# Projection with rotation by permutation, row mask inside the maximum, first loads moved ahead

## The chip, the cores and the metric

The kernel runs on one core of a Trainium2 chip. The metric is the device time in microseconds of one execution; lower is better. Engines are named as in the profile: PE is TensorE's matmul, PEld its weight load, DVE VectorE, ACT ScalarE, POOL GpSimd, SP SyncE.

## What is computed

One transformer layer over 4096 positions of width 256 in float32: causal attention with 16 heads of 16, rotary position encoding on queries and keys, then a gated feed-forward part with hidden width 1024, each followed by a layer norm.

```python
q, k, v = split_heads(x @ Wq.T + bq), split_heads(x @ Wk.T + bk), split_heads(x @ Wv.T + bv)
# rope: Y * cos + concat([-Y[..., d//2:], Y[..., :d//2]]) * sin
q, k = rope(q), rope(k)
att = softmax(where(tril, q @ k.T / sqrt(16), -inf))
x = layernorm(x + (att @ v) @ Wo.T + bo)
x = layernorm(x + ffn(x))
```

## The kernel before

The kernel is a sequence of blocks, each with its own programs for the five engines; a block starts when all engines have ended the one before. The blocks are `project`, `attend`, `widen` and `narrow`. The change touches the first two.

**`project`** (L57 to L235) works on 8 chunks of 512 positions. For each chunk it makes four column blocks of 128 features (two of the queries, two of the keys), transposed: features on partitions, positions along the free dimension. For each block PE makes two products from the chunk's x: the plain one and the rotated one, the latter with weights whose halves were exchanged and negated beforehand (`wqr`, `wkr`, made by DVE at L170 and L171). DVE then computes, in order and each step after the one before: `t1` = (plain + bias) x cos (L187), `t2` = (rotated + bias) x sin (L189), `full` = t1 + t2 (L193), and a split of `full` into three bfloat16 parts whose sum is `full` (L197 to L204). SP stores the three parts to HBM (L226). After every two blocks PE makes the values of half a chunk (L152), DVE adds their bias (L209), SP stores them (L230). Weights, biases and chunks are loaded on ACT's queue (L108 to L125). ACT computes nothing here, and GpSimd only fills the ones beside the values.

**`attend`** (L290 to L598) goes through four groups of four heads ("quads"), each with 8 chunks of queries. For one quad the queries and keys stand in SBUF as "stacks": six products of bfloat16 parts laid under one another (6 x 16 = 96 partitions), below them three partitions for the negated row maximum (queries) against ones (keys). There are two kinds of products. A row unit (`row_unit`, L454) has queries on partitions and up to 512 keys along the free dimension, and DVE reduces it to a maximum (`segment`, L531). A key unit (`key_unit`, L470) has keys on partitions, includes the subtraction of the maximum by the three extra partitions, and ACT exponentiates it (L595); its result is the moving operand of the product with the values (L489). Row units run ahead of key units by a number of columns that `rows_before_keys` lays down; the order on PE is written out by hand from it. Before the first key unit, 51 row units stand. Row units use a ring of four PSUM banks, key units of three.

A unit on the diagonal has a causal mask. In the row unit it is a second matmul of 128 columns that adds -1e30 in PSUM (L457, `mask` against `ident`); its width is 128, 256, 384 or 512 columns, depending on the tile (`row_width`). Key units have such a matmul too (L473).

When all row units of a chunk are done, `finish` (L534) splits the maxima into three parts (L541 is the first cast), PE transposes them (L448), and SP sends them through HBM into the query stack (`store_max`).

At the start of the block SP loads the stacks of the first chunk of quad 0 (twelve DMAs, `load_first`), the constants `ident` and `mask`, and the stacks of chunks 1 and 2. POOL loads the values, clears a pad of 15 columns (L367) and writes the ones into the key stacks by memset (L369), for both buffers in turn. PE waits for the casts of the constants (L558, L559) and for both pads. Later stacks of quad 0 are loaded by SP in the course of the block, three chunks ahead.

Of the kernel before, what the change touches and what calls it, by code (L numbers as in the profile page):

```python
# [18 lines left out]
F32 = mybir.dt.float32  # L19
F32R = mybir.dt.float32r  # L20
BF16 = mybir.dt.bfloat16
# [4 lines left out]
P = 128  # L26
# [22 lines left out]
FIRST_AHEAD = 3  # L49
# [7 lines left out]
def project(nc, io, qp_d, kp_d, v_d):  # L57

    with ExitStack() as ctx:
# [6 lines left out]
        wq = sb("wq", [P, DH, D])  # L66
        wk = sb("wk", [P, DH, D])
        wv = sb("wv", [P, DH, D])
        wqr = sb("wqr", [P, DH, D])
        wkr = sb("wkr", [P, DH, D])  # L70

        bias = sb("bias", [P, 4 * DH])
        sign = sb("sign", [P, 1])
        bv = sb("bv", [P, D])
        xt = sb("xt", [P, 2, DH, CH])
        cos = sb("cos", [P, 2, CH])
        sin = sb("sin", [P, 2, CH])
        t1 = sb("t1", [P, CH])
        t2 = sb("t2", [P, CH])
        full = sb("full", [P, CH])  # L80
        rest = sb("rest", [P, CH])
        parts = sb("parts", [P, 2, PARTS, CH], BF16)
        vals = sb("vals", [P, 2, 2, HEADS, VW])
        main_ps = [ctx.enter_context(nc.psum_tensor(f"pr_main{i}", [P, CH], F32)) for i in range(2)]
# [3 lines left out]
        weights_loaded = sem("weights_loaded")  # L88
        x_loaded = [sem(f"x_loaded{u}") for u in range(2)]
        tables_loaded = [sem(f"tables_loaded{u}") for u in range(2)]  # L90
        v_ones = sem("v_ones")
        weights_ready = sem("weights_ready")
        pair_ready = sem("pair_ready")
        pair_taken = sem("pair_taken")
        v_ready = sem("v_ready")
        v_taken = sem("v_taken")
        step = sem("step")
        parts_ready = sem("parts_ready")
        parts_stored = [sem(f"parts_stored{s}") for s in range(2)]
        v_stored = [sem(f"v_stored{s}") for s in range(2)]  # L100
        PAIRS = 2 * DH

        block = ctx.enter_context(nc.Block())

        @block.scalar
        def _(act):
            for dst, src in ((wq, "WqT"), (wk, "WkT"), (wv, "WvT")):
                act.dma_start(dst[:, :, :], io[src].rearrange("(c p) o -> p c o", p=P)).then_inc(weights_loaded, 16)  # L108
            act.dma_start(bias[:, :], io["bias"]).then_inc(weights_loaded, 16)
            act.dma_start(sign[:, :], io["sign"]).then_inc(weights_loaded, 16)  # L110
            act.dma_start(bv[:, :], io["bv"].partition_broadcast(P)).then_inc(weights_loaded, 16)

            def load(u, n):
                act.dma_start(xt[:, u, :, :], io["xT"][n]).then_inc(x_loaded[u], 16)
                act.dma_start(cos[:, u, :], io["cos"][n]).then_inc(tables_loaded[u], 16)
                act.dma_start(sin[:, u, :], io["sin"][n]).then_inc(tables_loaded[u], 16)

            load(0, 0)
            load(1, 1)
            with act.Fori(0, NCH // 2 - 1) as it:  # L120
                for u in range(2):

                    act.wait_ge(v_ready, it * 4 + 2 * u + 2)
                    act.wait_ge(pair_taken, it * 2 * PAIRS + PAIRS * (u + 1) + 2)
                    load(u, it * 2 + (2 + u))  # L125
# [4 lines left out]

        @block.tensor
        def _(pe):
            pe.wait_ge(weights_ready, 6)
            with pe.Fori(0, NCH // 2) as it:
                for u in range(2):
                    pe.wait_ge(x_loaded[u], it * 16 + 16)
                    for i, (w, wr) in enumerate(((wq, wqr), (wk, wkr))):
                        for half in range(DH):
                            cols = slice(half * P, (half + 1) * P)

                            pe.wait_ge(pair_taken, it * 2 * PAIRS + PAIRS * u + DH * i + half + 1)
                            for bank, weight in ((main_ps[half], w), (rot_ps[half], wr)):
                                for c in range(DH):
                                    last = nc.tensor.matmul(bank[:, :], weight[:, c, cols], xt[:, u, c, :],
                                                            start=(c == 0), stop=(c == DH - 1))
                            last.then_inc(pair_ready, 1)

                        pe.wait_ge(v_taken, it * 4 + 2 * u + i + 1)
                        for j in range(2):
                            tile = slice((2 * i + j) * P, (2 * i + j + 1) * P)  # L150
                            for c in range(DH):
                                last = nc.tensor.matmul(v_ps[i][:, j, :], xt[:, u, c, tile], wv[:, c, :],  # L152
                                                        start=(c == 0), stop=(c == DH - 1))
                        last.then_inc(v_ready, 1)

        @block.vector
        def _(dve):
            dve.sem_inc(pair_taken, 2)
            dve.sem_inc(v_taken, 2)
            dve.wait_ge(weights_loaded, 6 * 16)  # L160

# [53 lines left out]
        def _(sp):  # L215
            for s in range(2):
                sp.sem_inc(parts_stored[s], 48)
                sp.sem_inc(v_stored[s], 32)
# [1047 lines left out]
```

## Time and profile before

| | us |
|---|---|
| median of three runs | 2890.32 |
| lowest and highest | 2888.95, 2891.99 |
| profiled execution, its own time | 2888.47 |
| its span, first to last instruction | 2886.7 |

| stretch | what runs |
|---|---|
| 0 to 173.8 us | `project` |
| 173.8 to about 1800 | `attend` |
| from there to 2886.7 | end of `attend`, `widen`, `narrow` |

| engine | busy us | share of the span |
|---|---|---|
| PE | 2781.7 | 96% |
| DVE | 1944.8 | 67% |
| ACT | 1296.6 | 45% |
| POOL | 94.8 | 3% |

Times in the rows below are microseconds from the start of the span, unless a column says ns. An engine is busy while an instruction of it runs; matmuls overlap, and their ends are modelled, so a matmul's own duration is longer than the distance to the next one's start. ACTq and SPq are DMA issues of these queues. In brackets stands idle time before an instruction and what ended it.

### The profile page before, as it was taken

The page shows a single profiled execution, that of the slowest core. Times are in us where ns is not written, and L with a number is a line of the kernel's source. Part 1 is how long each engine was busy: PE and PEld are TensorE (multiplying, and loading weights), DVE is VectorE, ACT ScalarE, POOL GpSimd, SP SyncE. Part 2 cuts the span into 40 slices and gives each one's busy share as a digit, 9 for nine tenths or more (in the row PEclk, how much of TensorE's full clock was granted, in tenths as well). Part 3 has the DMA queues.
Part 4 walks back from the last instruction along what each step waited for, and adds up shares of the span by engine and source line. Part 5 has one row for each costly group of instructions (what it writes and reads, how often), then busy time and mean ns, then how long its engine had stood idle before and what let it go on. Part 6 is the DMA issues. An engine that isn't in the chain of part 4 may idle for free. (4 is left out here: it accounts for less than half of the span.)

```text
span 2886.7 us, 39857 instructions
## 1 busy us (share of the span) xinstructions
PE 2781.7 (96%) x15456; PEld 1474.2 (51%) x15456; DVE 1944.8 (67%) x3592; ACT 1296.6 (45%) x2545; POOL 94.8 (3%) x121
## 2 busy tenths in 40 slices
PE   8949999999999999999999999899999999999998
PEld 4423333333333333333333333388888887888887
DVE  7979999988888887888887776353333333344343
ACT  0005666677776676777777777511112111101100
POOL 0030100002000010000000000000000000000000
PEclk9969999999999999999999999999999999999999
DMA  5540270008000017000001000221111132112100
GB/s 155 166 106 27 45 89 3 3 2 103 7 3 4 5 28 91 3 3 3 3 3 38 18 4 8 75 71 56 57 59 64 48 124 111 44 44 87 44 15 23
DMA packets 94569, 132.89 MB, mean 46 GB/s; under 512 B 30688, under 2 KB 68192, under 8 KB 90688
## 3 DMA queue, kind: packets, MB, share of 16 engines
q1 hardware_dynamic: 83184, 96.91, 10.4%
q0 software_dynamic: 5472, 23.34, 6.5%
q10 hardware_dynamic: 5744, 10.36, 1.2%
q8 instruction: 110, 1.80, 0.3%
q14 instruction: 59, 0.48, 0.1%
HBM read 83.25 MB, written 47.32 MB: 45 GB/s over the span
## 5 line engine op out<-in xcount | busy, mean ns | idle before, releaser
L531 DVE TENSOR_REDUCE at_segmax<-at_row 128x1 f32<-128x512 f32 (+3 forms) x2304 | 1329.1, 638 | 236.2 <-PE at_row L454 178.3
L595 ACT ACTIVATE at_probs<-at_key 128x512 f32<-128x512 f32 (+3 forms) x2304 | 1130.9, 567 | 532.6 <-PE at_key L470 362.3
L454 PE MATMUL at_row<-fr_k_stack,fr_q_stack 96*128 96x512 bf16 (+3 forms) x1152 | 407.3, 374 | 32.2 <-POOL at_values L367 28.3
L470 PE MATMUL at_key<-fr_q_stack,fr_k_stack 99*128 99x512 bf16 (+3 forms) x1152 | 414.7, 364 | 2.7 <-ACT at_probs L595 2.7
L454 PE MATMUL at_row<-at_k_stack,at_q_stack 96*128 96x512 bf16 (+3 forms) x1152 | 412.1, 364 | 1.4 <-DVE at_segmax L531 1.2
L470 PE MATMUL at_key<-at_q_stack,at_k_stack 99*128 99x512 bf16 (+3 forms) x1152 | 402.8, 364 | 6.7 <-ACT at_probs L595 6.2
L489 PE MATMUL at_o<-at_probs,at_values 128*32 128x512 f32 (+3 forms) x2304 | 286.9, 570 | 0.0
L489 PE MATMUL at_o<-at_probs,fr_values 128*32 128x512 f32 (+3 forms) x2304 | 286.4, 569 | 0.0
L454 PEld LDWEIGHTS at_row<-fr_k_stack,fr_q_stack 96*128 96x128 bf16 x1152 | 112.1, 99 | 309.2 <-DVE at_segmax L531 202.1
L454 PEld LDWEIGHTS at_row<-at_k_stack,at_q_stack 96*128 96x128 bf16 x1152 | 112.0, 97 | 293.2 <-DVE at_segmax L531 211.1
L1128 ACT ACTIVATE na_h3f<-na_h,na_hs 128x512 f32<-128x512 f32 x64 | 44.1, 690 | 401.9 <-PE na_h L1098 401.9
L1098 PE MATMUL na_h<-na_h_h,fr_h2w_h 128*128 128x512 f32 x512 | 203.7, 398 | 5.4 <-DVE na_h_l L1143 5.4
L1098 PE MATMUL na_h<-na_h_l,fr_h2w_h 128*128 128x512 f32 x512 | 203.4, 397 | 0.0
L1098 PE MATMUL na_h<-na_h_h,fr_h2w_l 128*128 128x512 f32 x512 | 203.4, 397 | 0.0
L897 PE MATMUL wi_f<-wi_h_h,wi_h1w_h 128*128 128x512 f32 x512 | 201.4, 393 | 0.0
L897 PE MATMUL wi_f<-wi_h_l,wi_h1w_h 128*128 128x512 f32 x512 | 199.3, 389 | 0.0
L897 PE MATMUL wi_f<-wi_h_h,wi_h1w_l 128*128 128x512 f32 x512 | 199.3, 389 | 0.0
L1150 DVE CAST na_h_h<-na_h3f 128x512 fp32r<-128x512 f32 x64 | 27.3, 427 | 245.8 <-ACT na_h3f L1128 245.8
L941 ACT ACTIVATE wi_h<-wi_f,fr_hs 128x512 f32<-128x512 f32 x64 | 44.1, 689 | 324.6 <-PE wi_f L897 324.6
L470 PEld LDWEIGHTS at_key<-at_q_stack,at_k_stack 99*128 99x128 bf16 x1152 | 111.6, 98 | 146.9 <-ACT at_probs L595 78.8
L897 PE MATMUL wi_f<-fr_x1t,fr_w_h 128*128 128x512 f32 x512 | 160.8, 396 | 9.1 <-PEq L305 9.0
L470 PEld LDWEIGHTS at_key<-fr_q_stack,fr_k_stack 99*128 99x128 bf16 x1152 | 112.8, 98 | 94.7 <-ACT at_probs L595 27.8
(125 smaller groups left out, 2702.7 us busy)
## 6 DMA issues: line engine op xcount, KB each, us to landing
hidden<-wi_h SPq DMA_DIRECT2D x64, 256.0 KB, 2.0
na_h2f<-hidden SPq DMA_DIRECT2D x8, 1024.0 KB, 8.4
q_parts<-pr_parts SPq DMA_DIRECT2D x48, 128.0 KB, 1.9
k_parts<-pr_parts SPq DMA_DIRECT2D x48, 128.0 KB, 2.2
at_q_stack<-q_parts POOLq DMA_DIRECT2D x48, 128.0 KB, 23.8
at_k_stack<-k_parts POOLq DMA_DIRECT2D x12, 512.0 KB, 27.7
values<-pr_vals SPq DMA_DIRECT2D x32, 136.0 KB, 2.8
outputs<-at_outs SPq DMA_DIRECT2D x128, 34.0 KB
```

Of the source, the lines that this page charges most:

```text
L454: last = nc.tensor.matmul(bank[:, 0:w], qst[u][0:SROWS, c, h, i * P:(i + 1) * P], kst[u][0:SROWS, h, s * CH:s * CH + w], start=True, stop= ...
L470: last = nc.tensor.matmul(bank[:, q0:CH], kst[u][0:SROWS + PARTS, h, j * P:(j + 1) * P], qst[u][0:SROWS + PARTS, c, h, q0:CH], start=True, ...
L489: last = nc.tensor.matmul(o_ps[32 * h:32 * h + 32, q0:CH], vq[u][:, at:at + 32], probs[:, g % RING_P, h, q0:CH], start=(j == 0), stop=(g = ...
L531: nc.vector.tensor_reduce(segmax[:, n % 2, h * TPC + i, s:s + 1], row_ps[r % RING_R][:, 0:w], op=ALU.max, axis=AX.X).then_inc(rows_taken, 1)
L595: nc.scalar.activation(probs[:, g % RING_P, h, q0:CH], key_ps[m % RING_K][:, q0:CH], ACT.Exp).then_inc(probs_ready, 1)
L897: last = nc.tensor.matmul(bank[:, :], w[a][:, c, cols], moving(b, c), start=(m == 0), stop=(m == 3 * count - 1))
L941: nc.scalar.activation(h2[:, k % 2, :], fb[k % 4][:, :], ACT.Gelu, scale=front.hs[:, k:k + 1]).then_inc(hid_taken, 1)
L1098: last = nc.tensor.matmul(hb[k % 4][:, :], h2w[a][:, c, cols], h2[b][:, c, :], start=(m == 0), stop=(m == 3 * FK - 1))
L1128: nc.scalar.activation(h3f[:, k % 2, :], hb[k % 4][:, :], ACT.Gelu, scale=hs[:, k:k + 1]).then_inc(hid_taken, 1)
L1150: nc.vector.tensor_copy(h3[0][:, k, :], h3f[:, k % 2, :]).then_inc(h3_high, 1)
```

## The change

In `project`:

- The rotated product is no longer made from rotated weights. ACT makes `lin` = product x scale + bias from PSUM into SBUF, PE multiplies `lin` by a constant 128 x 128 matrix `turn` of 0, 1 and -1 that exchanges and negates the halves of each head, and the result is multiplied by sin.
- The work is spread over four engines and software-pipelined: ACT makes `lin` and the two bfloat16 casts, POOL makes `t1` = lin x cos, DVE makes `t2`, `rest`, `full` and the third part, one after the other for blocks g, g-1, g and g-2. The loops are written out.
- Chunks are loaded three deep, the stores have four slots. The loads at the start are spread over ACT's and SP's queues, x first on SP. `weights_ready` and the preparation on DVE go, but for the scaling of the query bias.
- The stacks of the first three chunks of quad 0 are loaded on ACT's queue during the projection (after blocks 4n+3 of chunks 2, 3 and 4), the constants and the ones of the first key stack on SP's queue at the start.

In `attend`: the ones of the second key stack are a DMA at the start of SP's queue, with the stack of the fourth chunk after it. The memsets of ones are gone. The row unit's mask matmul goes; on the diagonal DVE's reduction becomes `tensor_tensor_reduce`, which adds a constant tile `causal` and takes the maximum, and also writes the sum to `masked`, a double buffer. `FIRST_AHEAD` is 4 instead of 3.

```diff
@@ project, ScalarE @@
+            def linear(g):
+                m = g % UNITS
+                act.wait_ge(main_ready, g + 1)
+                if g >= 3:
+                    act.wait_ge(rot_ready, g - 2)
+                    act.wait_ge(t1_ready, g - 2)
+                nc.scalar.activation(lin[:, g % 3, :], main_ps[g % 3][:, :], ACT.Identity, bias=bias[:, m:m + 1],
+                                     scale=HD ** -0.5 if m < DH else 1.0).then_inc(lin_ready, 1)
...
+            linear(0)
+            for g in range(NU + 1):
+                if g + 1 < NU:
+                    linear(g + 1)
+                if g < NU:
+                    act.wait_ge(full_ready, g + 1)
...
+                    nc.scalar.activation(parts[:, g % SLOTS, 0, :], full[:, g % 2, :], ACT.Copy).then_inc(hi_ready, 1)
+                if g >= 1:
+                    act.wait_ge(rest_ready, g)
+                    nc.scalar.activation(parts[:, (g - 1) % SLOTS, 1, :], rest[:, (g - 1) % 2, :], ACT.Copy
+                                         ).then_inc(mid_ready, 1)
...
+                if m == 3 and 2 <= n < 2 + FIRST_EARLY:
+                    for slot in range(SLOTS):
+                        act.wait_ge(parts_stored[slot], 16 * PARTS * (n - 1))
+                    front.load_first(act, qp_d, kp_d, n - 2)
@@ project, TensorE @@
+            main(0)
+            for g in range(NU):
+                if g + 1 < NU:
+                    main(g + 1)
+                rotate(g)
+                if g % 2 == 1:
+                    values(g // UNITS, g % UNITS // 2)
@@ project, GpSimd @@
+            nc.gpsimd.memset(front.vq[:, NT * QUAD * VW:], 0.0).then_inc(front.pad_ready, 1)
...
+                nc.gpsimd.tensor_tensor(t1[:, g % 2, :], lin[:, g % 3, :], cos[:, n % BUFS, :], ALU.mult
+                                        ).then_inc(t1_ready, 1)
@@ project, VectorE @@
+                    nc.vector.tensor_tensor(t2[:, g % 2, :], rot_ps[g % 2][:, :], sin[:, n % BUFS, :], ALU.mult
+                                            ).then_inc(t2_ready, 1)
...
+                    nc.vector.tensor_tensor(rest[:, (g - 1) % 2, :], full[:, (g - 1) % 2, :], parts[:, (g - 1) % SLOTS, 0, :],
+                                            ALU.subtract).then_inc(rest_ready, 1)
...
+                    nc.vector.tensor_tensor(full[:, g % 2, :], t1[:, g % 2, :], t2[:, g % 2, :], ALU.add
+                                            ).then_inc(full_ready, 1)
@@ attend, GpSimd @@
             load_values(0, 0)
-            for u in range(2):
-                nc.gpsimd.memset(vq[u][:, NT * QUAD * VW:], 0.0).then_inc(pad_ready, 1)
-                pool.wait_ge(pad_ready, u + 1)
-                nc.gpsimd.memset(kst[u][SROWS:SROWS + PARTS, :, :], 1.0).then_inc(ones_ready[u], 1)
-                pool.wait_ge(ones_ready[u], 1)
+            nc.gpsimd.memset(vq[1][:, NT * QUAD * VW:], 0.0).then_inc(pad_ready, 1)
@@ attend, TensorE @@
-                                        kst[u][0:SROWS, h, s * CH:s * CH + w], start=True, stop=(s < c))
-                if s == c:
-                    last = nc.tensor.matmul(bank[:, w - P:w], mask[:, :], ident[:, :], start=False, stop=True)
+                                        kst[u][0:SROWS, h, s * CH:s * CH + w], start=True, stop=True)
@@ attend, VectorE @@
+                if s == blocks[n][1]:
+                    if diagonal[r] >= 2:
+                        dve.wait_ge(rows_taken, diagonal_at[diagonal[r] - 2] + 1)
+                    nc.vector.tensor_tensor_reduce(out=masked[:, diagonal[r] % 2, 0:w], in0=row_ps[r % RING_R][:, 0:w], in1=causal[:, CH - w:CH],
+                                                   scale=1.0, scalar=MASKED, op0=ALU.add, op1=ALU.max,
+                                                   accum_out=segmax[:, n % 2, h * TPC + i, s:s + 1]).then_inc(rows_taken, 1)
+                    return
```

## Rows read from the trace of the kernel before

**Rows 1.** The page's first part: busy us, share of the span, instructions.

```profile
PE 2781.7 (96%) x15456; PEld 1474.2 (51%) x15456; DVE 1944.8 (67%) x3592; ACT 1296.6 (45%) x2545; POOL 94.8 (3%) x121
```

**Rows 2.** Busy by stretch: length, PE, PEld, DVE, ACT, POOL, clock, DMA share, GB/s.

```profile
20.00:40.00 20.00, 20.00 (x57) 10.53 (x56) 19.14 (x34) 0.00 (x0) 0.00 (x0) 1.00 0.51 159
```

**Rows 3.** Groups by line, 0 to 200: busy us, mean ns, idle before.

```profile
L199 DVE TENSOR_TENSOR pr_rest<-pr_full,pr_parts 128x512 f32<-128x512 f32 x32 | 22.2, 693 | 1.1
...
L209 DVE TENSOR_TENSOR pr_vals<-pr_v,pr_bv 128x256 f32<-128x256 f32 x32 | 12.0, 415 | 0.0
```

**Rows 4.** Timeline, start of projection: start us, us, engine, line, operation.

```profile
3.75 0.45 ACTq L114 DMA_DIRECT2D pr_xt<-in_xT  x1
...
10.17 3.44 PE L144 MATMUL pr_main<-pr_xt,pr_wq 128*128 128x512 f32 x4 [10.17 <-DMA pr_xt<-in_xT]
...
15.16 1.88 PE L144 MATMUL pr_main<-pr_xt,pr_wq 128*128 128x512 f32 x4
...
15.37 0.75 DVE L187 SCALAR_TENSOR_TENSOR pr_t<-pr_main,pr_bias,pr_cos 128x512 f32<-128x512 f32 x1 [5.28 <-PE pr_rot L144]
...
16.03 0.74 DVE L189 SCALAR_TENSOR_TENSOR pr_t<-pr_rot,pr_bias,pr_sin 128x512 f32<-128x512 f32 x1
...
16.88 1.88 PE L144 MATMUL pr_rot<-pr_xt,pr_wqr 128*128 128x512 f32 x4
...
24.98 0.74 DVE L187 SCALAR_TENSOR_TENSOR pr_t<-pr_main,pr_bias,pr_cos 128x512 f32<-128x512 f32 x1
```

**Rows 5.** Timeline, from the last projection matmul to the first rows.

```profile
159.16 1.89 PE L152 MATMUL pr_v<-pr_wv,pr_xt 128*128 128x256 f32 x8
...
169.85 0.95 SPq L230 DMA_DIRECT2D values<-pr_vals  x2
...
173.82 0.36 SPq L390 DMA_DIRECT2D fr_q_stack<-q_parts  x1
...
175.27 13.75 POOL L369 MEMSET fr_k_stack<- 3x16384 bf16 x1
...
180.67 0.67 SPq L410 DMA_DIRECT2D fr_ident<-in_ident  x1
...
189.27 13.75 POOL L369 MEMSET at_k_stack<- 3x16384 bf16 x1
...
189.31 0.27 PE L454 MATMUL at_row<-fr_k_stack,fr_q_stack 96*128 96x128 bf16 x1 [28.27 <-POOL at_values L367]
...
196.66 6.39 DVE L541 CAST at_maxparts<-at_negmax 128x16 bf16<-128x16 f32 x1
...
203.29 0.17 DVE L545 CAST at_maxparts<-at_maxrest 128x16 bf16<-128x16 f32 x1
```

**Rows 6.** Busy by stretch of attention, columns as in group 2.

```profile
189.00:220.00 31.00, 22.46 (x88) 8.99 (x88) 30.21 (x57) 0.16 (x1) 13.90 (x3) 0.56 0.24 54
220.00:395.00 175.00, 168.57 (x1051) 59.80 (x1049) 168.57 (x320) 109.59 (x218) 16.27 (x31) 0.98 0.35 52
395.00:1800.00 1405.00, 1391.84 (x8831) 474.18 (x8831) 1168.78 (x2124) 996.25 (x2033) 32.56 (x63) 1.00 0.12 19
```

**Rows 7.** The same for the mask matmuls alone (L457): PE, PEld, clock, DMA.

```profile
189.00:220.00 31.00, 9.58 (x33) 4.50 (x33) 0.56 0.24 54
220.00:395.00 175.00, 14.25 (x64) 6.37 (x63) 0.98 0.35 52
395.00:1800.00 1405.00, 90.82 (x416) 40.83 (x416) 1.00 0.12 19
```

**Rows 8.** Timeline, steady attention.

```profile
1101.48 2.48 DVE L531 TENSOR_REDUCE at_segmax<-at_row 128x1 f32<-128x512 f32 x4 [0.55 <-PE at_row L454]
...
1101.72 0.22 PE L457 MATMUL at_row<-at_ident,at_mask 128*128 128x128 bf16 x1
...
1101.76 2.06 ACT L595 ACTIVATE at_probs<-at_key 128x512 f32<-128x512 f32 x4 [0.61 <-PE at_key L470]
1101.78 0.38 PE L470 MATMUL at_key<-fr_q_stack,fr_k_stack 99*128 99x512 bf16 x1
```

More of the change, by code:

```diff
@@ L80, in project @@
-        full = sb("full", [P, CH])
-        rest = sb("rest", [P, CH])
-        parts = sb("parts", [P, 2, PARTS, CH], BF16)
+        w = [sb(f"w{a}", [P, DH, D]) for a in "qkv"]
+        turn = sb("turn", [P, P])
+        bias = sb("bias", [P, UNITS])
+        bv = sb("bv", [P, D])
+        xt = sb("xt", [P, BUFS, DH, CH])
+        cos = sb("cos", [P, BUFS, CH])
+        sin = sb("sin", [P, BUFS, CH])
+        lin = sb("lin", [P, 3, CH])
+        t1 = sb("t1", [P, 2, CH])
+        t2 = sb("t2", [P, 2, CH])
@@ new lines, in _, with main, rotate, values @@
+        @block.tensor
+        def _(pe):
+            def main(g):
+                n, m = divmod(g, UNITS)
+                if m == 0:
+                    pe.wait_ge(x_loaded[n % BUFS], 16 * (n // BUFS + 1))
+                if n == 0 and m % DH == 0:
+                    pe.wait_ge(w_loaded[m // DH], 16)
+                if g >= 3:
+                    pe.wait_ge(lin_ready, g - 2)
+                cols = slice((m % DH) * P, (m % DH + 1) * P)
+                for c in range(DH):
+                    last = nc.tensor.matmul(main_ps[g % 3][:, :], w[m // DH][:, c, cols], xt[:, n % BUFS, c, :],
+                                            start=(c == 0), stop=(c == DH - 1))
+                last.then_inc(main_ready, 1)
+            def rotate(g):
+                if g == 0:
+                    pe.wait_ge(turn_loaded, 16)
+                if g >= 2:
+                    pe.wait_ge(t2_ready, g - 1)
+                pe.wait_ge(lin_ready, g + 1)
+                nc.tensor.matmul(rot_ps[g % 2][:, :], turn[:, :], lin[:, g % 3, :], start=True, stop=True).then_inc(rot_ready, 1)
+            def values(n, i):
+                if n == 0 and i == 0:
+                    pe.wait_ge(w_loaded[2], 16)
+                if n > 0:
+                    pe.wait_ge(v_taken, 2 * (n - 1) + i + 1)
+                for j in range(2):
+                    tile = slice((2 * i + j) * P, (2 * i + j + 1) * P)
+                    for c in range(DH):
+                        last = nc.tensor.matmul(v_ps[i][:, j, :], xt[:, n % BUFS, c, tile], w[2][:, c, :],
+                                                start=(c == 0), stop=(c == DH - 1))
+                last.then_inc(v_ready, 1)
+            main(0)
[5 more added lines that the diff above has]
+                    values(g // UNITS, g % UNITS // 2)
@@ L129, in _ @@
             nc.gpsimd.memset(vals[:, :, :, :, :], 1.0).then_inc(v_ones, 1)
[L131 to L154, printed above, removed]
@@ L238, in attend_plan @@
+            for s in range(SLOTS):
+                sp.wait_ge(parts_stored[s], 16 * PARTS * NU // SLOTS)
+            for i in range(2):
+                sp.wait_ge(v_stored[i], 32 * NCH)
 def attend_plan():
@@ L299, in attend @@
     out_after = {min(g + 1, NG - 1): n for n, g in last_group.items()}
+    diagonal_at = [r for r, (n, i, _, s) in enumerate(rows) if i != TURN and s == blocks[n][1]]
+    diagonal = {r: k for k, r in enumerate(diagonal_at)}
     MR = PARTS * QUAD * TPC
@@ L1192 @@
     "WqT": [D, D], "WkT": [D, D], "WvT": [D, D], "WoT": [D, D],
-    "bias": [P, 4 * DH], "sign": [P, 1], "bv": [D], "bo": [D],
-    "ident": [P, P], "mask": [P, P],
+    "bias": [P, 2 * DH], "turn": [P, P], "bv": [D], "bo": [D],
+    "ident": [P, P], "mask": [P, P], "causal": [P, CH], "ones": [PARTS, QUAD * T // 2],
     "w1T": [D, F], "w2T": [D, F], "h1T": [F, F], "h2T": [F, F], "w3T": [F, D],
```

282 lines of the change are left out of this document (145 added, 137 removed).

## Prediction

> **What bounds the kernel now.** I read the page's busy table first [rows 1]. TensorE is counted busy for nearly the whole span, but that is an average over stages, so I went on to the busy time by stretches and to the timeline of each stage that the diff touches.
>
> In the projection (0 to 173.8 us) the bound is VectorE: 19.14 of 20 us busy in a steady stretch [rows 2]. The timeline gives the beat. The first product of one pair of column blocks is taken at 15.37, that of the next pair at 24.98, so a pair costs 9.61 us [rows 4], and 16 pairs 153.8 us. TensorE needs less: a two-chunk product and its rotated twin start 16.88 - 15.16 = 1.72 us apart, and the eight value records run 1.89 us with starts that fill about 1.72 [rows 4, 5]. That is 4 x 1.72 + 1.72 = 8.6 us per pair.
>
> The turn to attention costs much. The last projection matmul ends at 161.05, the attention block starts at 173.82, and its first row product at 189.31 [rows 5]. There it waits for the second 15-column memset, which is queued on GpSimd behind the 13.75 us memset of ones. While the second memset of ones runs (189.27 to 203.02) a cast of 16 columns on VectorE takes 6.39 us and ends at 203.05. The same kind of cast afterwards takes 0.17 us [rows 5].
>
> In attention there are three parts. Up to 220 us only row products run: VectorE is busy 30.21 of 31 us. From 220 to 395 it is idle for 6.4 us. From 395 to 1800 it is idle for 236 us, and TensorE is the bound [rows 6]. What follows attention is untouched.
>
> **Projection, VectorE side.** Removed: two fused operations, two casts and the weight preparation. Left per column block: four tensor-tensor operations and the values. Fused ones start 0.66 us apart at 0.75 us each [rows 4], a plain one runs 0.693 [rows 3], so I put its pace at 0.61. 4 x 0.61 + 0.375 (values, [rows 3]) = 2.8 us per block.
>
> **Projection, TensorE side.** The rotated product (two chunks, 1.72) becomes one chunk with the permutation, 0.86. Per block 1.72 + 0.86 + 0.86 (half the values of a pair) = 3.44 us, 110.1 us for 32 blocks. TensorE becomes the bound.
>
> **ScalarE** gets three passes per block. Four exponentials take 2.06 us [rows 8], so a pass has a pace near 0.5 and a length up to 0.6: at most 1.8 of 3.44 us. But it also issues DMAs in order. The twelve of one first stack took 180.67 - 173.82 = 6.85 us on SyncE [rows 5], and in the changed kernel they stand on ScalarE between a split pass and the next bias pass, three times. TensorE can go on for about 1.4 us past that point before it needs the next biased block (three buffers), so each costs 4.1 to 5.5 us. I take 4.7, 14 us in all. The three loads of a chunk (some 1.5 us) just fit.
>
> **GpSimd** gets the product with the cosine. The trace has no wide two-input operation there. Lower bound: memset's 0.84 ns per column [rows 5], 0.43 us. Upper bound: the 3.44 us of a block, above which it would set the beat. I take about 1 us, twice the memset and a fixed part, since two inputs are nearest to twice one. It then hides. It can delay VectorE where both use the same path to SBUF, as the 6.39 us cast shows [rows 5]. I add 3 us for slips.
>
> The Trainium skill, "SBUF — State Buffer", section "Who interferes with whom", states more: a VectorE instruction with two SBUF inputs and a GpSimd instruction that reads SBUF exclude each other for the whole instruction. The trace agrees only for a cast against a memset (6.39 us), not for such a pair. By that rule VectorE would lose up to 1 us per block; this is rival C. "GPSIMD Engine Reference", section 3.1, gives 4497 ns for 2048 columns of a two-input add; an estimate of 1.1 us for 512 follows, and the sum would not change by it.
>
> **Start and end of the projection.** The first chunk's load is issued at 3.75 and TensorE starts at 10.17, after VectorE's preparation [rows 4]. The load moves to the head of SyncE's queue, 3 us earlier, and the preparation goes: start at 5 to 7, I take 6. The first product still runs at half clock, 3.44 instead of 1.72 us [rows 4]: +1.7. TensorE ends at 6 + 110.1 + 1.7 + 14 + 3 = 134.8. Behind it the last block's chain (four VectorE steps with two ScalarE passes between), five issues and a landing follow. Before it took 12.8 us [rows 5]. With more overlap I take 9, giving a block start at 143.8.
>
> **Turn to attention.** Both memsets of ones are DMAs now, the constants and three first stacks are there. What remains is two casts and a 15-column memset behind the issue of the value load: 1.5 us instead of 15.5. First row product at 145.3 instead of 189.3: **-44.0**. The stalled cast falls to 0.17: **-6.2**. SyncE's new start work (ones and the fourth stack, about 6 us) lies beside the first rows.
>
> **Row mask inside the maximum.** Of 513 mask matmuls, 33 lie before 220 us, 64 from there to 395, 416 later [rows 7]. On TensorE each is 1101.78 - 1101.72 = 0.06 us [rows 8]. On VectorE the reduction becomes an operation with two inputs, a 320-column mean output and an accumulator. Lower end of its extra: a fused operation's pace (0.66) against a reduction's 0.60 to 0.62 (2.48 for four, [rows 8]), so 0.05. Upper end: a second pass over the columns, 0.375 at that pace, so 0.43. I take 0.2: 0.05 and one small separate operation to write the accumulator, like the 0.17 us casts [rows 5]. The Trainium skill, "VectorE: DVE Perf Modes", section "Two Vector instructions with no wait between them", says that an operation that also writes its accumulator is two instructions. No row shows it.
> Where VectorE is the bound this is paid: 33 x 0.2 = **+6.6**. In 220 to 395, 12.8 less part of the 6.4 idle: **+10**. Later 416 x 0.2 = 83 us fits in 236 us of idle, and TensorE gains 416 x 0.06 = 25. Since diagonal rows come in clusters in the short blocks, where the ring of four banks makes TensorE wait, I credit three quarters: **-18.7**.
>
> **Sum.** -44.0 - 6.2 + 6.6 + 10 - 18.7 = -52.3. The profiled execution took 2888.5, so 2836.2. The median of the runs lies 1.8 above it: 2838.
>
> **Rivals.**
> B. The masked maximum is cheap (extra near 0.06) and ScalarE's stalls smaller. 97 x 0.14 = 13.6 less: about 2822. For it: fused operations with a PSUM input run at full column rate [rows 4]. Against: the accumulator has to be written.
> C. GpSimd and VectorE shut each other out in the projection. VectorE's 2.8 plus up to 1 to 1.2 us gives 3.8 to 4.0 per block against 3.44, 32 x 0.56 = 18: about 2856. For it: the 6.39 us cast. Against: it is seen with a cast only, and two of VectorE's five operations read PSUM.
> D. The masked maximum costs about 0.3 more. 97 x 0.1 = 10, and TensorE's 18.7 is lost to waits on the ring: about 2867.
> E. **Slower.** The masked maximum goes over its columns twice or drains between its parts, extra 0.43. Before 395 us: 97 x 0.43 - 6.4 = 35. Later 416 x 0.43 = 179 us, of which perhaps half the idle (118) absorbs a part: +61. With -50.2 from the front that is +46, 2936. It decides at 97e - 6.4 + 416e - 118 = 50.2, e = 0.34. Against it: the fused operations' 0.75 us for 512 columns [rows 4] is one pass.
> F. The front's gain is not realised: the first stacks are late or the earlier start only moves the time into VectorE's row phase. But that phase has a fixed count of rows, so an earlier first row moves all of it. Near 2888.
>
> **How the numbers follow.** Forecast 0.50 (own range 2824 to 2852), B 0.17, C 0.17, D 0.08, E 0.06, F 0.02. Eight in ten: 2815 to 2867 takes in the forecast, most of B, C and part of D. Within 0.2% is about what a measurement of this kernel can tell from no change. Faster 0.92, same 0.02, slower 0.06.
>
> **What would show each step.** Attention's block starting near 144 us and its first row product 1.5 us later. TensorE at 6.9 us per pair in the projection, with three gaps of 4 to 5 us before a permutation product, where ScalarE issues twelve DMAs. VectorE below 90% there; if it is full and its two-SBUF-input operations are stretched to 1.3 us or more, it is C. The casts of 16 columns all near 0.17. The mean of the masked maximum near 0.2 above the reduction of the same width, and VectorE's idle time after 395 us down to about 150. The prediction is wrong if GpSimd's product takes over 2 us, if the masked maximum costs over 0.3 more, or if TensorE in attention waits for row banks.

## The result, and the profile after

| | before | after |
|---|---|---|
| median us | 2889.64 (4 runs, 2888.95 to 2891.99) | 2842.13 (4 runs, 2841.43 to 2843.42) |
| span of the profiled execution | 2886.7 | 2841.3 |
| its own time | 2888.47 | 2843.42 |

The ratio is 0.9835, with an interval of 0.9821 to 0.9848. The kernel is 47.5 us faster; the profiled executions' spans differ by 45.4. All ratios below are against the kernel before. The forecast was 2838, within 2815 to 2867.

The page's first part, kernel after (busy us, share, instructions), and under it the busy time by stretches: length, PE, PEld, DVE, ACT, POOL, granted clock, DMA share, GB/s.

```profile
PE 2742.2 (97%) x14880; PEld 1433.1 (50%) x14880; DVE 1902.1 (67%) x4001; ACT 1350.8 (48%) x2641; POOL 112.3 (4%) x151
...
20.00:40.00 20.00, 20.00 (x60) 11.03 (x59) 19.91 (x27) 9.84 (x18) 8.42 (x6) 1.00 0.61 179
...
145.00:176.00 31.00, 22.56 (x55) 5.71 (x55) 25.04 (x93) 0.60 (x1) 0.90 (x2) 0.50 0.53 109
176.00:351.00 175.00, 158.54 (x932) 52.55 (x933) 158.16 (x356) 101.52 (x204) 16.23 (x31) 0.94 0.42 61
351.00:1755.00 1404.00, 1385.67 (x8470) 451.71 (x8468) 1183.46 (x2564) 1001.10 (x2046) 32.50 (x63) 0.99 0.11 17
```

The first stretch answers to [rows 2]. ScalarE and GpSimd now carry part of the projection, and both TensorE and VectorE read as full. The last three are those of [rows 6], moved 44 us earlier. The middle one is the surprise: TensorE was idle for 6.4 us there, now it is idle for 16.5.

The turn from projection to attention, timeline of the kernel after (start us, us, engine, line, operation), answering to [rows 5]:

```profile
135.12 1.89 PE L153 MATMUL pr_v<-pr_wv,pr_xt 128*128 128x256 f32 x8
...
142.01 3.00 SPq L283 DMA_DIRECT2D k_parts<-pr_parts  x6
...
145.05 1.06 SPq L289 DMA_DIRECT2D values<-pr_vals  x2
...
149.03 0.23 DVE L611 CAST at_ident<-fr_ident 128x128 bf16<-128x128 f32 x1 [6.83 <-PEq L65]
...
150.68 6.14 PE L501 MATMUL at_row<-fr_k_stack,fr_q_stack 96*128 96x128 bf16 x18 [13.66 <-POOL at_values L428]
...
155.16 0.08 DVE L580 DVE_READ_ACCUMULATOR2_ANT at_segmax<- 128x1 f32 x1
155.16 0.69 DVE L580 CUSTOM_DVE_ANT_0 fr_masked<-at_row,fr_causal 128x512 f32<-128x512 f32 x1
...
155.77 0.69 DVE L580 CUSTOM_DVE_ANT_0 fr_masked<-at_row,fr_causal 128x512 f32<-128x512 f32 x1
...
157.94 0.17 DVE L594 CAST at_maxparts<-at_negmax 128x16 bf16<-128x16 f32 x1
```

The first row product stands at 150.68 instead of 189.31, the cast that took 6.39 us takes 0.17, and two masked maxima of 512 columns start 0.61 us apart.

To see where the rest went I followed the ends of the 32 attention blocks (a quad's chunk each, numbered from 0), as the first copy of its output on ScalarE shows them:

| end of block | before | after | gained so far |
|---|---|---|---|
| first row product | 189.31 | 150.68 | 38.6 |
| 0 | 240.74 | 195.84 | 44.9 |
| 2 | 307.44 | 263.86 | 43.6 |
| 3 | 356.01 | 323.09 | 32.9 |
| 31 | 1851.73 | 1806.27 | 45.5 |

So the start gave 38.6 and the cast 6.2. A small loss of 1.3 follows in block 2 (experiment 2 tells whose it is). Then **10.7 us were lost inside block 3**, which the prediction does not have. From there to the end 12.6 came back.

### The profile page after: what moved, and what is told of

Read it like the earlier page. It is cut to its first block and busy times, and to the rows that moved or that the text cites. A ratio compares the mean times of both kernels' runs of the same rounds, so it can differ in the third digit from the quotient of the medians.

```text
span 2841.3 us, 39343 instructions
## 1 busy us (share of the span) xinstructions
PE 2742.2 (97%) x14880; PEld 1433.1 (50%) x14880; DVE 1902.1 (67%) x4001; ACT 1350.8 (48%) x2641; POOL 112.3 (4%) x151
## 5 line engine op out<-in xcount | busy, mean ns | idle before, releaser
L584 DVE TENSOR_REDUCE at_segmax<-at_row 128x1 f32<-128x512 f32 x1792 | 1143.1, 684 | 183.6 <-PE at_row L501 179.6
L580 DVE CUSTOM_DVE_ANT_0 fr_masked<-at_row,fr_causal 128x384 f32<-128x384 f32 (+3 forms) x512 | 243.9, 483 | 49.3 <-PE at_row L501 48.7
## 6 DMA issues: line engine op xcount, KB each, us to landing
at_q_stack<-q_parts POOLq DMA_DIRECT2D x48, 128.0 KB, 23.6
```

What stands on the lines that cost most here:

```text
L580: nc.vector.tensor_tensor_reduce(out=masked[:, diagonal[r] % 2, 0:w], in0=row_ps[r % RING_R][:, 0:w], in1=causal[:, CH - w:CH], scale=1.0, ...
L584: nc.vector.tensor_reduce(segmax[:, n % 2, h * TPC + i, s:s + 1], row_ps[r % RING_R][:, 0:w], op=ALU.max, axis=AX.X).then_inc(rows_taken, 1)
```

## The experiments

**1. Where block 3 lost its time.** Timelines of the kernel after: GpSimd's queue, SyncE's queue, TensorE; then the busy time of a stretch.

```profile
254.20 2.16 POOL L420 DMA_DIRECT2D at_q_stack<-q_parts  x4 [103.81 <-DMA fr_k_stack<-k_parts]
...
293.59 0.31 SPq L445 DMA_DIRECT2D maxima<-at_maxrows  x1
317.36 0.23 SPq L449 DMA_DIRECT2D fr_q_stack<-maxima  x1
...
319.12 0.61 PE L515 MATMUL at_key<-fr_q_stack,fr_k_stack 99*128 99x512 bf16 x1 [9.45 <-DMA fr_q_stack<-maxima]
...
264.00:304.00 40.00, 38.89 (x222) 12.19 (x221) 39.80 (x87) 26.75 (x51) 6.43 (x13) 1.00 1.03 112
```

GpSimd waits for the last first stack of quad 0 and then issues the whole load of quad 1. The DMA engines are full from 264 to 304. The maxima of block 3 are stored at 293.59, and the next step on SyncE can only go at 317.36: of that, 23.4 us is waiting for this small store to land. In the kernel before, an undisturbed one was followed by its next step 1.4 us later (467.02, 468.41). TensorE stands for 9.45 us at the key product that needs it, and its next products run 0.61 to 0.63 instead of 0.38. The first edit sets `FIRST_AHEAD` back, so that the last stack is loaded a block later. The second, further down, keeps it at 4 and lets GpSimd also wait for six maxima stores.

```diff
-FIRST_AHEAD = 4
+FIRST_AHEAD = 3
```

> The changed kernel, but first stacks of quad 0 are loaded three chunks ahead in attention, as before the change. Theory A (bulk load collides): the 30 DMAs of the next quad's stacks, released when the last first stack is in, start at 254 us in the changed kernel and fill all queues while the maxima of chunk 4 are to be stored; that store took 23.4 us instead of 1.4 and TensorE stood 9.4 us. With three ahead the bulk load starts one block later, and the collision meets the store of chunk 5, which had 14 us of slack in the kernel before: 10 to 11 us faster than the changed kernel, about 2832. Rival B (the 10.7 us at the fourth block come from VectorE, which carries the masked maxima): no change, 2842.

Measured: 2824.12 (2823.1 to 2826.43), ratio 0.9773 (0.976 to 0.9786), 18 us below the kernel after. Block 3 ends at 311.64, 11.45 earlier, though block 2 ended only 0.4 earlier. The same two queues in this kernel:

```profile
303.71 2.16 POOL L420 DMA_DIRECT2D at_q_stack<-q_parts  x4 [153.69 <-DMA fr_k_stack<-k_parts]
...
351.43 0.31 SPq L445 DMA_DIRECT2D maxima<-at_maxrows  x1
366.20 0.23 SPq L449 DMA_DIRECT2D fr_q_stack<-maxima  x1
```

The load still makes a maxima store slow (14.4 us), but at a block where it is early enough: no wait on TensorE is left. In the kernel before it was also there: stored at 396.39, next step at 410.25, unseen. So the collision is shown, and 11 of the 18 us are its price. The expected time was 2832; the other 7 us are taken up in experiment 6.

```diff
             pool.wait_ge(first_loaded[NCH - 1], 12 * 16)
+            pool.wait_ge(max_spilled, 16 * 6)
             load(1, 1)
```

> The changed kernel with one wait more on GpSimd: the bulk load of the next quad's stacks starts only when the maxima of chunk 5 have been stored, so that its 60 us fall between two stores of maxima. Theory A: the stores take 1.4 us each, 10 to 12 us faster than the changed kernel, 2830 to 2832, and not slower than with three chunks ahead. Rival B (VectorE's maxima): 2842. A third case: the bulk load then comes too late for the first row products of the second quad, and the time is above 2842.

Measured: 2824.92 (2821.7 to 2826.35), ratio 0.9771 (0.9758 to 0.9785). The load is issued at 354.18, and from 250 to 420 us no maxima store waits more than 1.0 us. The time is that of the first edit: once the slow landing is off the path, removing it altogether is worth nothing more.

**2. The masked maximum against the mask on TensorE.** On top of experiment 1's first edit, the old mask matmul and the plain reduction come back, and all else stays.

```diff
-                                        ..., start=True, stop=True)
+                                        ..., start=True, stop=(s < c))
+                if s == c:
+                    last = nc.tensor.matmul(bank[:, w - P:w], mask[:, :], ident[:, :], start=False, stop=True)
@@ VectorE @@
-                if s == blocks[n][1]:
...
-                    nc.vector.tensor_tensor_reduce(out=masked[...], in0=row_ps[...], in1=causal[:, CH - w:CH], ...)
-                    return
```

> As e1_ahead3, and the row mask back in TensorE's matmul (the masked maximum undone). This gives the price of that part alone, free of the collision. By the trace of the changed kernel the masked maximum costs VectorE 0.08 us more than a reduction (the accumulator read) and saves TensorE 0.06: 97 x 0.08 = 8 lost where VectorE is the bound, 416 x 0.057 = 24 gained where TensorE is. So this kernel should be 10 to 20 us slower than e1_ahead3. The recorded prediction's terms (0.2 us on VectorE, three quarters of TensorE's gain) say 2 us slower. Rival (clusters of diagonal rows eat the gain): equal within 3 us.

Measured: 2843.35 (2841.95 to 2846.08), ratio 0.9842 (0.9828 to 0.9855). The masked maximum is worth 19.2 us by the medians (16.5 by the spans of the profiled executions). Groups by form over attention, first of the kernel after, then of this one (busy us, mean ns, idle before):

```profile
L580 DVE CUSTOM_DVE_ANT_0 fr_masked<-at_row,fr_causal 128x512 f32<-128x512 f32 x128 | 86.8, 683 | 12.5 <-PE at_row L501 12.5
...
L580 DVE DVE_READ_ACCUMULATOR2_ANT at_segmax<- 128x1 f32 x512 | 42.3, 83 | 0.0
```

```profile
L579 DVE TENSOR_REDUCE at_segmax<-at_row 128x1 f32<-128x512 f32 x1920 | 1215.2, 682 | 195.9 <-PE at_row L501 176.6 <-PE at_row L504 14.8
```

The narrower forms agree as well: 550, 417 and 282 ns masked, 549, 416 and 281 plain, for 384, 256 and 128 columns. The separate read of the accumulator (83 ns) runs in the last part of the operation: the next one still starts 0.61 us after the one before, as a plain reduction does (0.60 to 0.62, [rows 8]). So the extra on VectorE is 0.01 us at most. Block ends of this kernel and of experiment 1's first tell where the gain lies: from first row product to first exponential 24.3 against 24.4 us, no difference; from the end of block 3 to the end of the last, 18.0 us (18.7 if experiment 1's first kernel is compared with the kernel before).

The 1.3 us of block 2 are not the masked maximum's either. Here is the stretch from the end of block 0 to the end of block 2, of the kernel before, of the kernel after and of this one (the column before the last two is the granted clock):

```profile
240.74:307.44 66.70, 63.29 (x412) 22.37 (x411) 63.47 (x123) 40.93 (x83) 0.00 (x0) 1.00 0.10 30
195.84:263.86 68.02, 63.94 (x386) 20.74 (x386) 63.87 (x150) 40.71 (x84) 9.66 (x19) 0.97 0.24 44
193.75:261.98 68.23, 64.88 (x412) 22.60 (x411) 63.58 (x123) 40.92 (x83) 0.00 (x0) 0.97 0.11 29
```

With the mask back on TensorE the stretch is 1.5 us longer than before, at the same lower clock. So before the end of block 3 no cost of the masked maximum is seen at all.

**3. ScalarE's stalls in the projection.** The stall that the prediction named, timeline of the kernel after:

```profile
54.07 0.34 ACTq L723 DMA_DIRECT2D fr_q_stack<-q_parts  x1
...
59.34 0.45 ACTq L724 DMA_DIRECT2D fr_k_stack<-k_parts  x1
59.91 0.69 ACT L180 ACTIVATE pr_lin<-pr_main,pr_bias 128x512 f32<-128x512 f32 x1 [4.88 <-issue]
...
60.74 2.05 PE L143 MATMUL pr_rot<-pr_lin,pr_turn 128*128 128x512 f32 x2 [5.38 <-ACT pr_lin L180]
```

Twelve issues take 5.7 us, the bias pass follows, TensorE waits 5.38 us, and its next two products take 2.05 us instead of 1.02: from 62 to 66 us the granted clock is 0.50, which is 1.2 of 2.4 GHz. With nothing else changed, the first stacks are issued on SyncE, in portions behind the stores of each block.

```diff
@@ project, ScalarE @@
-                if m == 3 and 2 <= n < 2 + FIRST_EARLY:
...
-                    front.load_first(act, qp_d, kp_d, n - 2)
@@ project, SyncE, behind the stores of a block @@
+                if 2 <= n < 2 + FIRST_EARLY:
+                    if m == 0:
+                        for slot in range(SLOTS):
+                            sp.wait_ge(parts_stored[slot], 16 * PARTS * (n - 1))
+                    front.load_first(sp, qp_d, kp_d, n - 2, ((0, 1), (2,), (3, 4), (5,))[m])
...
```

> The changed kernel with the first three stacks issued on SyncE's queue during the projection, a few DMAs after each block's stores, instead of twelve at once on ScalarE. Theory C (in-order ScalarE: bias passes wait behind twelve issues): TensorE's three stalls of 5.4, 3.2 and 3.2 us go, and with them the stretches at half clock behind them: projection 12 to 18 us shorter, 2824 to 2830 in all. Rival D (the DMA engines are full there, and the stalls would come back as waits for stores on SyncE): less than 5 us, 2838 to 2842.

Measured: 2831.78 (2830.33 to 2834.26), ratio 0.9801 (0.9788 to 0.9815), 10.3 us below the kernel after: less than was expected, since the projection became 9.8 us shorter and not 12 to 18. The table of waits, first the projection, then 225 to 325 (us in total, times, longest):

```profile
PE pr_rot L143 <- ACT pr_lin L180: 5.8, 7, 1.2
...
SPq L449 <- DMA maxima<-at_maxrows: 24.4, 2, 23.4
```

The first line is of this kernel; in the kernel after it reads 12.3 us, four times, longest 5.4. The second is of the kernel after and is the same here (24.5, longest 23.4): this edit leaves the collision alone. Attention starts at 139.2 instead of 149.0, so 9.8 us at the turn: 6.5 of waiting, and the rest is put down to the clock, which reads 1.00 from 5 to 128 us here and 0.94 in the kernel after.

**4. Do VectorE and GpSimd shut each other out?** Groups by line in the projection, kernel after (busy us, mean ns, idle before), answering to [rows 3]:

```profile
L225 POOL TENSOR_TENSOR pr_t<-pr_lin,pr_cos 128x512 f32<-128x512 f32 x32 | 45.1, 1411 | 88.5 <-ACT pr_lin L180 88.5
...
L253 DVE TENSOR_TENSOR pr_parts<-pr_rest,pr_parts 128x512 bf16<-128x512 f32 x32 | 33.6, 1049 | 0.1
...
L244 DVE TENSOR_TENSOR pr_rest<-pr_full,pr_parts 128x512 f32<-128x512 f32 x32 | 28.2, 882 | 0.0
...
L249 DVE TENSOR_TENSOR pr_full<-pr_t 128x512 f32<-128x512 f32 x32 | 23.1, 723 | 0.1
L238 DVE TENSOR_TENSOR pr_t<-pr_rot,pr_sin 128x512 f32<-128x512 f32 x32 | 21.8, 681 | 26.0 <-PE pr_rot L143 26.0
```

One pair of them in the timeline, and the beat:

```profile
123.32 0.68 DVE L238 TENSOR_TENSOR pr_t<-pr_rot,pr_sin 128x512 f32<-128x512 f32 x1
...
125.02 1.32 POOL L225 TENSOR_TENSOR pr_t<-pr_lin,pr_cos 128x512 f32<-128x512 f32 x1 [3.37 <-ACT pr_lin L180]
...
125.12 1.76 DVE L253 TENSOR_TENSOR pr_parts<-pr_rest,pr_parts 128x512 bf16<-128x512 f32 x1
...
130.20 0.68 DVE L238 TENSOR_TENSOR pr_t<-pr_rot,pr_sin 128x512 f32<-128x512 f32 x1
```

The product of GpSimd ends at 126.34, the operation of VectorE 0.54 later: it did its columns after the product, not beside it. Line 238, whose first input lies in PSUM, is never stretched. The three lines with two inputs in SBUF together cost (1049 + 882 + 723 - 3 x 681) = 611 ns per block. Yet a pair takes 130.20 - 123.32 = 6.88 us, exactly TensorE's 2 x 3.44, and both engines read full there (from 110 to 130 us, 20.00 of 20 us each). Two kernels tell this apart: a second GpSimd product per block whose result nobody reads, and, as a control, a memset of 1536 columns in its place. Both stand ahead of the needed product and are built on experiment 1's first kernel.

```diff
+                nc.gpsimd.tensor_tensor(dump[:, g % 2, 0:CH], lin[:, g % 3, :], cos[:, n % BUFS, :], ALU.mult)
                 nc.gpsimd.tensor_tensor(t1[:, g % 2, :], lin[:, g % 3, :], cos[:, n % BUFS, :], ALU.mult
@@ or, in the control @@
+                nc.gpsimd.memset(dump[:, g % 2, :], 0.0)
...
```

> As e1_ahead3, and GpSimd makes its product with the cosine twice per column block in the projection, the first time into a tile that nobody reads. In the changed kernel GpSimd's product takes 1.27 us, and VectorE's operations with two SBUF inputs are stretched from 0.68 to 1.0 to 1.76 us exactly while it runs. Theory L (the two exclude each other for the whole instruction): VectorE has 2.8 us of own work per block, of which 1.0 reads PSUM and can overlap, plus 2.55 of GpSimd: 4.4 to 5.4 us against TensorE's 3.44. The projection grows by 30 to 60 us, 2854 to 2884 in all. Rival M (the stretch is only a shared rate, or delay in the chain): GpSimd is busy 2.6 of 3.44 us, and the time grows by less than 6 us, under 2830.

> Control for e5_pool_twice: instead of the second product a memset of 1536 columns, which at the memset rate seen (0.84 ns per column) takes about 1.3 us, the same as the product, but reads nothing. It delays the real product by the same time. Theory L (exclusion holds against GpSimd instructions that read): VectorE's operations overlap with the memset, and the time stays within 4 us of e1_ahead3, 2820 to 2830. Rival M' (any GpSimd work excludes VectorE, or the later product lengthens the chain): as slow as e5_pool_twice.

Measured with the second product: 2848.2 (2845.04 to 2852.02), ratio 0.9849 (0.9836 to 0.9862); attention starts at 167.5, 18.8 us after experiment 1's 148.7. That is far above the under 2830 of the rival, and below the 2854 to 2884 of the exclusion as it was priced. With the memset: 2833.63 (2828.69 to 2836.71), ratio 0.9796 (0.9782 to 0.981); start at 154.3, 5.7 later, and in the median 3.6 us above what was expected. Groups by line of the first:

```profile
L251 DVE TENSOR_TENSOR pr_full<-pr_t 128x512 f32<-128x512 f32 x32 | 39.9, 1247 | 0.5 <-POOL pr_t L227 0.5
L255 DVE TENSOR_TENSOR pr_parts<-pr_rest,pr_parts 128x512 bf16<-128x512 f32 x32 | 35.7, 1117 | 0.1
L246 DVE TENSOR_TENSOR pr_rest<-pr_full,pr_parts 128x512 f32<-128x512 f32 x32 | 34.0, 1063 | 0.1
L240 DVE TENSOR_TENSOR pr_t<-pr_rot,pr_sin 128x512 f32<-128x512 f32 x32 | 21.8, 680 | 20.4 <-PE pr_rot L144 20.2
```

and the timeline of the control:

```profile
122.95 1.38 POOL L226 MEMSET pr_dump<- 128x1536 f32 x1 [2.37 <-ACT pr_lin L181]
...
123.45 0.68 DVE L255 TENSOR_TENSOR pr_parts<-pr_rest,pr_parts 128x512 bf16<-128x512 f32 x1
```

The stretch grows from 611 to 1247 + 1117 + 1063 - 3 x 681 = 1384 ns per block. VectorE then needs 2.8 + 1.38 = 4.2 us per block on average, against TensorE's 3.44. From 120 to 140 us it is busy 20.00 of 20 us and TensorE 17.34: now VectorE sets the beat, and GpSimd with its 3.1 us does not. Over the whole projection a block grows by 18.8 / 32 = 0.59 us, less than the difference of the two sums. A memset of 1.38 us, as long as a product, leaves a two-input operation at 0.68 us: 24 of them ran beside a memset and no product, and none took over 0.69, and the control's stretch is 640 ns per block, near the 611. So the loss comes from the pair of operations, not from GpSimd's being busy. Two things came with it. In the kernel after, VectorE's sum is about 2.8 + 0.61 = 3.4 us per block (an estimate, since the 2.8 is put together from paces), as much as TensorE's 3.44, so the exclusion of rival C is there but stays hidden, with no margin left. And the control is not free: its product is later, and waits at the permutation grow from 11.8 to 15.5 us. So a part of the 18.8 us, up to the control's 5.7, is the later product and not the exclusion.

The Trainium skill, "SBUF — State Buffer", section "Who interferes with whom", says that a VectorE instruction with two SBUF inputs contends with a GpSimd instruction that reads SBUF, and not with one that only writes it. The trace agrees: 1.76 us beside a product, 0.68 beside a memset.

**5. The best combination, and the projection's end.** Experiment 1's first edit and experiment 3's together.

> e1_ahead3 and e4_spfirst together: first stacks three ahead in attention, the first three stacks issued by SyncE in portions. If the collision of the bulk load (18 us) and ScalarE's blocked queue (10 us) are independent, 2842 - 18 - 10 = 2814. If SyncE's portions only shift the bulk load into another store of maxima, 2820 or above.

Measured: 2819.92 (2818.54 to 2821.73), ratio 0.9752 (0.9739 to 0.9764). It beats both kernels: 22 us below the kernel after, 71 below the one before. It was expected at 2814. Attention starts at 140.71, 7.9 us earlier than with the first edit alone, but the span is only 4.3 us shorter. The block ends tell where the rest went: 1.3 us in block 1, 1.0 from block 17 to block 19 and 2.3 in blocks 29 and 30, each at a lower granted clock than in the other kernel (block 1: 0.94 against 1.00, block 19: 0.93 against 0.96, both over the same number of matmuls; around blocks 29 and 30: 0.94 against 1.00). No maxima store delays TensorE here, so it is not the collision moved elsewhere. On top, the last block's three stores go to ScalarE's queue, to shorten the end of the projection:

```diff
+            act.wait_ge(parts_ready, NU)
+            for a in range(PARTS):
+                act.dma_start(kp_d[a, (DH - 1) * P:DH * P, NCH - 1, :], parts[:, (NU - 1) % SLOTS, a, :]
+                              ).then_inc(parts_stored[(NU - 1) % SLOTS], 16)
...
```

> As e7_ahead3_sp, and the three stores of the last column block go out on ScalarE's queue, which is idle then, beside SyncE's. In e4_spfirst SyncE issues the last parts from 131.97 to 134.97 and the last values until 136.07, and attention starts at 139.2. With 1.4 us of issues off that queue the start of attention moves by 1.4 us: 1 to 2 us faster than e7_ahead3_sp, about 2812. If the landing of the stores and not the issuing ends the block: no change.

Measured: 2822.18 (2815.8 to 2824.81), ratio 0.9754 (0.974 to 0.9769): no difference. SyncE's last issue ends at 136.8 instead of 137.7, and attention starts at 140.71 in both. So the issuing on SyncE does not end the block. What is left between the last issue and the start is the landing of the last stores, 3.0 us in the one kernel and 3.9 in the other; that it ends the block is argued, not shown.

**6. The ones by memset, and the clock.** On experiment 1's first kernel the two loads of ones become the old GpSimd memsets in attention.

```diff
+            nc.gpsimd.memset(kst[0][SROWS:SROWS + PARTS, :, :], 1.0).then_inc(ones_loaded[0], 1)
+            pool.wait_ge(ones_loaded[0], 1)
             nc.gpsimd.memset(vq[1][:, NT * QUAD * VW:], 0.0).then_inc(pad_ready, 1)
+            pool.wait_ge(pad_ready, 1)
+            nc.gpsimd.memset(kst[1][SROWS:SROWS + PARTS, :, :], 1.0).then_inc(ones_loaded[1], 1)
...
```

> As e1_ahead3, but the ones of both key stacks are written by GpSimd's memsets at the start of attention, as in the kernel before, with the pads in the same order. All else is as in the changed kernel. Theory T (the turn is bound by these memsets): the first row product again comes 15.5 us after the start of attention instead of 1.6, and the first split of the maxima is again held by the second memset, about 6 us: 18 to 21 us slower than e1_ahead3, 2842 to 2845. Rival (the loads of constants and first stacks at the start of attention were as much to blame, so the memsets alone cost less): less than 10 us slower, under 2834.

Measured: 2849.21 (2848.43 to 2852.45), ratio 0.9856 (0.984 to 0.9873), 25.1 us above experiment 1 (23.8 by the spans), and so above the 18 to 21 that were expected. Its timeline:

```profile
151.54 13.75 POOL L427 MEMSET fr_k_stack<- 3x16384 bf16 x1
...
165.51 13.75 POOL L431 MEMSET at_k_stack<- 3x16384 bf16 x1
165.71 6.13 PE L504 MATMUL at_row<-fr_k_stack,fr_q_stack 96*128 96x128 bf16 x18 [27.78 <-POOL at_values L429]
...
172.97 6.32 DVE L597 CAST at_maxparts<-at_negmax 128x16 bf16<-128x16 f32 x1
```

The first memset holds the first row product until 15.4 us after the block's start (150.3), the second holds the cast for 6.32. With a block start 1.6 us later that makes 21.6 us at the end of block 0 (21.2 at the end of block 3), and these are the two terms of the prediction. A further 3.1 us appears in block 11, and such a piece also explains what experiment 1 left open. Busy time in stretches (the column before the last two is the granted clock): two of the kernel after, then two of experiment 1's first kernel, over the same blocks, 11 and 19.

```profile
858.74:922.90 64.16, 59.48 (x359) 20.51 (x357) 53.07 (x182) 40.40 (x82) 0.00 (x0) 0.95 0.02 5
1093.44:1140.86 47.42, 46.28 (x264) 14.76 (x265) 34.37 (x67) 31.60 (x66) 0.00 (x0) 0.89 0.02 7
```

```profile
847.11:908.16 61.05, 56.37 (x359) 19.54 (x357) 52.65 (x182) 40.01 (x83) 0.00 (x0) 1.00 0.02 5
1078.93:1123.25 44.32, 43.18 (x264) 14.21 (x265) 33.87 (x67) 31.18 (x65) 0.00 (x0) 0.96 0.02 7
```

The work is the same, 359 and 264 matmuls, and each stretch is 3.1 us longer at the lower clock: 0.95 x 64.16 = 61.0 and 0.89 x 47.42 = 42.2 against 1.00 x 61.05 and 0.96 x 44.32 = 42.5. Two of them are 6.2 of experiment 1's 18 us. Ahead of the stretch at block 19 TensorE stood for 2.95 us in one kernel and 3.18 in the other. In block 11 its longest single waits were 1.26, 1.07 and 1.06 us in both. Why the clock fell in one and not in the other, and stayed down longer at block 19, no run settles.

What the wait ahead of block 19 is, the trace does tell: a second collision of the same kind. SyncE's queue, ScalarE and TensorE of the kernel after:

```profile
1058.36 20.18 SPq L456 DMA_DIRECT2D outputs<-at_outs  x4
...
1093.44 0.60 ACT L639 ACTIVATE at_outs<-at_o 128x512 f32<-128x512 f32 x1 [2.78 <-DMA outputs<-at_outs]
...
1094.58 0.61 PE L515 MATMUL at_key<-fr_q_stack,fr_k_stack 99*128 99x512 bf16 x1 [2.95 <-ACT at_probs L648]
```

GpSimd issues the bulk load of the last quad from 1029.02 on, and the DMA engines are full again (share 1.02 from 1060 to 1080). Issuing the four output stores of a block, mostly done in 1.3 us, takes 20.18 us here; ScalarE waits for them before it may take the next output, and TensorE waits for ScalarE. It is no work of the change: in the kernel before the same wait is 1.63 us on ScalarE. No run moved this load, so what it costs is not measured.

## Why the prediction was right

The total came out 4 us under the measured median (7 by the sums below; the profiled executions lie on different sides of their medians). The steps balance less well. Both columns are us against the profiled execution before; the later 18.7 is read from experiment 1 (gained 44.4 at the end of block 3, 63.1 at the end of the last), the clock is what is left of the kernel after.

| step | predicted | measured |
|---|---|---|
| first row product | -44.0 | -38.6 |
| stalled cast | -6.2 | -6.2 |
| masked maxima before block 3 | +16.6 | none seen |
| clock in block 2 | none | +1.3 |
| maxima store behind the bulk load | none | +10.7 |
| later, mask matmuls gone | -18.7 | -18.7 |
| later, clock | none | +6.2 |
| sum | -52.3 | -45.3 |

**Start and beat.** TensorE starts at 5.16 (forecast 6), the beat is 6.88 us per pair where no wait stands in it, to the hundredth what was worked out from [rows 4]. It ends at 137.0 instead of 134.8: the waits at the permutation are 12.3 of the forecast 14, but the clock falls behind each long one, which the sum had only for the first product.

**Tail.** It takes 12.0 us, not 9. I expected the overlap to shorten the 12.8 of before; eight issues (142.01 to 146.11), where five had been counted, and 2.9 us until the block starts stand behind VectorE's last chain, and experiment 5 shows that fewer issues on SyncE would not help. The projection's later end (2.2 us), the tail (3.0) and the turn (0.2) make up the 5.4 us.

**Turn.** 1.7 us from block start to first row, against 1.5. The two prices of the memsets, 15.4 and 6.3, come back when the memsets do.

**Masked maximum.** The step that failed is its extra of 0.2 us. It is at most 0.01, since the read of the accumulator lies in the end of the operation before it. Rival B had this right (0.06). The Trainium skill, "VectorE: DVE Perf Modes", section "Two Vector instructions with no wait between them", makes it two instructions. The trace agrees (0.69 and 0.08 us), but the second costs no time. The term fell from 16.6 us to nothing that can be seen, and this paid for the collision. VectorE's idle time says the same: from 395 to 1800 us it is 249.7 us and not the 150 that the prediction expected. The credit of 18.7 for the later blocks was met, here (18.7) and in experiment 2 (18.0).

**What the prediction left out.** It costed the fourth stack's twelve issues on SyncE, and did not follow who waits for the last stack: GpSimd, with the bulk load of the next quad behind its wait. `FIRST_AHEAD = 4` moved that load from 347.91 to 254.20, 50 us earlier than the 44 us shift explains, into the path of a store that a key product needs.

**Rivals.** C's mechanism is real and came at 0.61 us per block, where its bound was 1, and TensorE's beat just covered it. The sign that the prediction gave for C (VectorE full, operations stretched to 1.3 us or more) was met, with 20.00 of 20 us and 1.76 us, and yet the time is not C's: the sign did not ask how many operations are stretched. D and E are excluded by the 0.01 us. F's claim is refuted by block 0, which ends 44.9 us earlier. Nearest in time is the forecast itself, but by errors of both signs: 16.6 us too dear (the early masked maxima), 23.6 too cheap (start and tail 5.4, collision 10.7, clock 1.3 and 6.2). It was a right number with wrong entries on both sides, and that they cancelled to 7 us was luck.

## What to carry to other kernels

When a change loads something earlier, follow every wait on that load, down to the bulk transfer that stands behind it, and look at which small transfer will then be in flight. In a balanced pipeline compare the engines' sums per block: a stretch of 0.6 us was free only because another engine needed as much time for its own block. DMA issues belong on a queue whose engine nobody on the beat waits for.

## What the runs showed of the hardware

- A reduction fused with an addition, with an accumulator and a full output, runs at the plain reduction's pace at every width: 282, 417, 550 and 683 ns for 128 to 512 columns.
- GpSimd and VectorE exclude each other in both directions. A VectorE operation with two SBUF inputs takes 0.68 us alone and up to 1.76 beside a GpSimd product; the product takes 1.27 us alone and up to 1.76 when it starts behind such an operation.
- With the DMA engines full, the step behind one small store could go 23.8 and 20.3 us after its issue, against 1.4 where they were not.
- TensorE's waits of 5.38, 3.23, 9.45, 2.95 and 3.18 us were each followed by products at half clock, and so cost more than the wait. After waits of some 1 us the clock fell in one kernel and not in another. In block 2 it fell in the kernel after and in experiment 2's (0.97 over 68 us), where the nearest waits ahead of it were 0.69 and 0.57 us, and not in the kernel before, where one of 0.57 us stands at the same place.
